# Query rotation moved to channel-major with half swaps by DMA, and the FFN input transposed by DMA, in a pre-norm attention + FFN block

## What is computed

```python
h = layernorm(x)
q, k, v, g = h @ Wq.T, h @ Wk.T, h @ Wv.T, h @ Wg.T        # each [.., 128], 8 heads of 16
q, k = rope(q), rope(k)                                    # z*cos + rotate_half(z)*sin
kv, ksum, vsum = sum_s k_s v_s^T, sum_s k_s, sum_s v_s     # per head, over the 256 tokens
num = q @ kv * scale + vsum
den = q @ ksum * scale + 256
o = (num / den + depthwise_conv5(v) + b) * g
x = x + o @ Wo.T
h2 = layernorm(x).bfloat16
y = e4m3fn(h2 / s_in) @ e4m3fn(W / s_k) * (s_in * s_k)     # FFN: one 128x128 product
out = x + bf16(y) + bias
```

## Time and profile before

| | before |
|---|---|
| median of 3 runs | 174.56 us (174.33 to 174.72) |
| the profiled execution | 174.49 us |
| its span, first to last instruction | 172.7 us |
| mean granted PE clock | 0.985 |
| PE, DVE, ACT, POOL busy | 94%, 88%, 77%, 80% of the span |
| HBM read, written | 5.25 MB, 4.19 MB |

### The profile page before, as it was taken

The page is one execution under the profiler, slowest core; times in us unless marked ns, Lnnn a source line. Parts: engine busy times, 40 slices in busy tenths (PEclk is TensorE's granted clock), DMA queues, the critical chain, the costliest instruction groups (busy, mean ns, idle before and its releaser), DMA issues.

```text
span 172.7 us, 3890 instructions
## 1 busy us (share of the span) xinstructions
PE 162.4 (94%) x1140; PEld 137.7 (80%) x1140; DVE 152.2 (88%) x281; ACT 132.5 (77%) x358; POOL 137.4 (80%) x163
## 2 busy tenths in 40 slices
PE   7999999999999999999999999999999999999730
PEld 2578988887879898998889898988998898978510
DVE  2298899989898999999899999989899899899944
ACT  3759757787987878896969888887787786667770
POOL 1468987777897888989898898996889875979871
PEclk9999999999999999999999999999999999999985
DMA  4930002004040404021030404040310220020224
GB/s 133 272 83 0 0 6 61 2 4 121 2 121 6 121 0 123 4 65 56 16 111 0 121 6 121 6 121 0 92 35 0 65 61 4 0 65 2 61 61 121
DMA packets 18966, 9.71 MB, mean 56 GB/s; under 512 B 1536, under 2 KB 18816, under 8 KB 18944
## 3 DMA queue, kind: packets, MB, share of 16 engines
q1 hardware_dynamic: 18368, 9.19, 18.6%
q10 hardware_dynamic: 576, 0.26, 0.6%
HBM read 5.25 MB, written 4.19 MB: 55 GB/s over the span
## 4 chain that ended last, share of the span: by engine, by line
PE 85%; POOL 4%; DVE 3%; issue 3%; ACT 2%; DVEq 0%; POOLq 0%; ACTq 0%
PE bank L1126 15%; PE bank L1210 9%; PE bank L1172 8%; PE p_num L1191 8%; PE bank L1137 8%; PE p_num L1183 8%; PE bank L1145 7%; PE bank L1161 4%; PE bank L1200 4%; PE bank L1116 4%; PE bank L1153 4%; PE bank L1083 3%; PE bank L1253 2%; PE bank L1219 2%; DVE yc L786 1%
## 5 line engine op out<-in xcount | busy, mean ns | idle before, releaser
L597 POOL TENSOR_TENSOR qk<-turned 128x512 f32<-128x512 f32 x32 | 40.3, 1274 | 3.1 <-DVE turned L826 2.9
L826 DVE TENSOR_TENSOR turned<-bank,turn 128x1024 f32<-128x1024 f32 x32 | 38.7, 1216 | 0.9 <-PE bank L1126 0.9
L841 DVE SCALAR_TENSOR_TENSOR acc<-bank,conv_w,acc 128x510 f32<-128x510 f32 (+1 forms) x48 | 34.8, 725 | 0.2
L1126 PE MATMUL bank<-w_qk,hT 128*128 128x256 f32 x128 | 32.8, 381 | 0.2
L370 ACT ACTIVATE h<-x,nmr,rs 128x128 bf16<-128x128 f32 x60 | 24.7, 485 | 3.9 <-POOL nmr L571 3.9
L306 ACT ACTIVATE h<-xs,nmr,rs 128x128 f32<-128x128 f32 x64 | 26.3, 484 | 0.6 <-POOL nmr L560 0.4
L557 POOL TENSOR_TENSOR rs<-ve,minus_half 128x4 f32<-128x4 f32 (+1 forms) x17 | 16.7, 980 | 12.5 <-ACT ve L297 12.5
L1126 PEld LDWEIGHTS bank<-w_qk,hT 128*128 128x128 f32 x128 | 22.6, 190 | 2.9 <-issue 0.3
L568 POOL TENSOR_TENSOR rs<-ve,minus_half 128x4 f32<-128x4 f32 (+1 forms) x17 | 16.6, 977 | 6.7 <-ACT ve L361 6.6
L609 POOL TENSOR_TENSOR acc<-acc,outer 128x508 f32<-128x508 f32 x16 | 20.3, 1271 | 1.0 <-DVE acc L841 1.0
L1137 PEld LDWEIGHTS bank<-w_v,hT 128*128 128x128 f32 x128 | 16.4, 191 | 4.7 <-issue 3.3
(11 more groups left out here) (88 smaller groups left out, 326.6 us busy)
## 6 DMA issues: line engine op xcount, KB each, us to landing
xs<-_attn_hidden_states_dram SPq DMA_DIRECT2D x15, 256.0 KB, 2.8
out_dram<-ob SPq DMA_DIRECT2D x15, 256.0 KB, 2.5
turn<-in_turn_dram SPq DMA_DIRECT2D x1, 512.0 KB, 4.7
xs<-_attn_hidden_states_dram SPq DMA_DIRECT2D x2, 128.0 KB, 2.8
out_dram<-ob SPq DMA_DIRECT2D x2, 128.0 KB, 2.1
mask<-in_mask_dram SPq DMA_DIRECT2D x1, 68.0 KB, 5.0
w_raw<-in_L_attn_Wq_dram ACTq DMA_DIRECT2D x1, 64.0 KB, 2.3
w_raw<-in_L_attn_Wk_dram ACTq DMA_DIRECT2D x1, 64.0 KB, 2.5
```

What stands on the lines that cost most here:

```text
L597: nc.gpsimd.tensor_tensor(qk[:, u % 2, j].rearrange("p q t d -> p t q d"), turned[:, j, :, :, 0:D].rearrange("p a h (q d) -> p (a h) q d", ...
L826: nc.vector.tensor_tensor(turned[:, j], p_qk[j].rearrange("p a h d -> p a (h d)").unsqueeze(2).to_broadcast([P, TPB, 2, 2 * D]), turn[:], ...
L841: nc.vector.scalar_tensor_tensor(out=part, in0=p_vT[:, :, lo + off:hi + off], scalar=conv_w[:, k:k + 1], in1=part, op0=ALU.mult, op1=ALU.a ...
L1126: last = nc.tensor.matmul(p_qk[j][:, a].rearrange("p h d -> p (h d)"), hT[:, u % 3, t * P:(t + 1) * P], w_qk[:].rearrange("p a q d -> p (a ...
```

## The change

q and k are no longer projected together. q is projected channel-major in one 128x512 product, like the gate, and rotated there. The two halves of a rotated pair now lie on different partitions (0 to 63 and 64 to 127), so DVE writes both products (z*cos and z*sin) and SP swaps the partition halves of the second by two DMAs from SBUF to SBUF (128 KB each); POOL adds them straight into `qT`. `transpose_q` and `move_qT` are gone. k stays token-major, in four 128x128 products. The table of 512 KB is loaded as two tables of 256 KB. For units 0 to 13 the bf16 `h2` (128x512, 128 KB) is transposed by a DMA of SP into a new SBUF tile `h2T`, which ACT (or DVE on the wide path) reads in place of PSUM; units 14 and 15 still use PE. The banks of PSUM are assigned anew, and the orders of all five queues are new. The code up to the orders, cut to its core:

```diff
+            def swap_q(u):
+                s = u % 2
+                sp.wait_ge(q_turned_done, count(u))
+                sp.dma_start(q_swapped[0:P // 2, s], q_turned[P // 2:P, s, 1]).then_inc(q_swapped_in[s], 16)
+                sp.dma_start(q_swapped[P // 2:P, s], q_turned[0:P // 2, s, 1]).then_inc(q_swapped_in[s], 16)
+
+            def turn_h2(u):
+                s = u % 2
+                sp.wait_ge(h2_done, count(u))
+                if u >= 2:
+                    sp.wait_ge(q8_done, count(u, 2))
+                sp.dma_start(h2T[:, s].rearrange("p (t k) -> p t k", t=TPU), h2[:, s].rearrange("p t d -> p (t d)"),
+                             transpose=True).then_inc(h2T_in[s], 16)
...
-            def move_qT(u):
...
-                    act.wait_ge(h2T_filled, count(u))
+                    if u < PE_H2:
+                        act.wait_ge(h2T_in[u % 2], h2T_count(u))
+                    else:
+                        act.wait_ge(h2T_filled, 1)
...
-            def add_rope(u, j):
...
+            def add_q(u):
+                s = u % 2
+                pool.wait_ge(q_swapped_in[s], 32 * (u // 2 + 1))
+                if u >= 2:
+                    pool.wait_ge(num_filled, count_last(u, 2))
+                nc.gpsimd.tensor_tensor(qT[:, s], q_turned[:, s, 0], q_swapped[:, s], ALU.add).then_inc(qT_done, 1)
+
+            def add_k(u):
+                s = u % 2
+                pool.wait_ge(k_turned_done, count(u))
+                if u >= 2:
+                    pool.wait_ge(kv_filled, count(u, 2))
+                nc.gpsimd.tensor_tensor(k[:, s], k_turned[:, s, :, :, 0:D // 2], k_turned[:, s, :, :, D // 2:D],
+                                        ALU.add).then_inc(k_done, 1)
...
-            def rope(u, j):
...
+            def turn_q_unit(u):
...
+                nc.vector.tensor_tensor(
+                    q_turned[:, s].rearrange("p c (j s) -> p c j s", j=BPU),
+                    p_q[:].rearrange("p (j s) -> p j s", j=BPU).unsqueeze(1).to_broadcast([P, 2, BPU, S]),
+                    turn_q[:].unsqueeze(2).to_broadcast([P, 2, BPU, S]), ALU.mult).then_inc(q_turned_done, 1)
+
+            def turn_k_unit(u):
...
+                nc.vector.tensor_tensor(
+                    k_turned[:, s].rearrange("p (j a) h d -> p j a h d", j=BPU),
+                    p_k.rearrange("p (j a) d -> p j a d", j=BPU).unsqueeze(3).to_broadcast([P, BPU, TPB, 2, D]),
+                    turn_k[:].unsqueeze(1).to_broadcast([P, BPU, TPB, 2, D]), ALU.mult).then_inc(k_turned_done, 1)
...
-            def project_qk(u, j, *freed):
+            def project_q(u, *freed):
...
+                nc.tensor.matmul(p_q[:], w_qk[:, 0].rearrange("p a d -> p (a d)"), hT[:, u % 3], start=True,
+                                 stop=True).then_inc(q_filled, 1)
+
+            def project_k(u, *freed):
...
+                for t in range(TPU):
+                    last = nc.tensor.matmul(p_k[:, t], hT[:, u % 3, t * P:(t + 1) * P],
+                                            w_qk[:, 1].rearrange("p a d -> p (a d)"), start=True, stop=True)
+                last.then_inc(k_filled, 1)
```

The middle of the orders, of PE, DVE, ACT, POOL and SP in turn:

```diff
             for t in range(7, 13):
                 project_g(t - 3, (x2_done, count_last(t - 4)))
-                project_v(t - 1, (hT_done, count_first(t - 1)))
-                project_qk(t - 1, 1, (rope_done[1], count(t - 2)))
-                transpose_t1(t - 3, (qT_done, count(t - 3)))
-                transpose_h2(t - 4, (v_done, count(t - 1)))
+                key_value(t - 2, (kvs_done, count(t - 3)))
+                transpose_t1(t - 3, (hT_done, count_first(t - 1)))
+                project_v(t - 1, (yb_done, count(t - 5)))
+                project_k(t - 1, (k_turned_done, count(t - 2)))
                 transpose_v(t - 1, (tap_done[-1], count(t - 2)))
-                key_value(t - 2, (rope_done[0], count(t - 2)))
-                ffn(t - 4, is_small, (q8_done, count(t - 4)))
-                transpose_q(t - 2, (t2_done, count_last(t - 3)))
+                project_q(t - 1, (v_done, count(t - 1)))
                 project_o(t - 3, (oT_done, count_last(t - 3)))
                 sum_v(t - 2, (t1_done, count_last(t - 3)))
-                project_qk(t - 1, 0, (kvs_done, count(t - 2)))
-                transpose_h(t, (yb_done, count(t - 4)))
                 attend(t - 2)
+                ffn(t - 4, is_small, (q_turned_done, count(t - 1)))
+                transpose_h(t, (t2_done, count_last(t - 3)))
...
+            for t in range(5, 12):
+                mask_kv(t - 2)
+                add_lepe(t - 3)
                 stats1(t)
-                add_lepe(t - 3)
                 gate(t - 3)
-                rope(t - 1, 1)
-                mask_kv(t - 2)
+                turn_k_unit(t - 1)
+                turn_q_unit(t - 1)
                 quantise_if_wide(t - 4, is_small)
                 residual(t - 3)
+                conv_tap(t - 1, 0)
                 stats2(t - 3)
...
+            for t in range(9, 12):
                 norm2(t - 4)
                 move_v(t - 1)
-                quantise_if_small(t - 4, is_small)
                 var_eps1(t)
                 conv_middle(t - 1)
+                conv_outer(t - 1)
+                quantise_if_small(t - 4, is_small)
+                norm1(t)
+                var_eps2(t - 3)
                 move_y(t - 4)
-                conv_outer(t - 1)
-                norm1(t)
-                move_qT(t - 2)
-                var_eps2(t - 3)
                 move_hT(t)
...
+            for t in range(9, 12):
+                add_k(t - 2)
+                pow2(t - 4)
                 add_bias(t - 5)
+                add_q(t - 2)
                 final_sum(t - 5)
+                pow1(t)
+                sum_outer(t - 2)
...
+            load_x(9)
+            swap_q(7)
+            turn_h2(5)
+            store(4)
+            load_x(10)
+            swap_q(8)
+            store(3)
+            turn_h2(6)
```

More of the change, by code:

```diff
@@ L217, in build @@
         h2T_filled = sem("h2T_filled")
+        h2T_in = [sem(f"h2T_in{n}") for n in range(2)]
         q8_done = sem("q8_done")
@@ L945, in _ @@
             conv_tap(2, 2)
+            turn_k_unit(3)
+            turn_q_unit(3)
             dve.wait_ge(w_ready, 1)
```

777 lines of the change are left out of this document (413 added, 364 removed).

## The result

The changed kernel was timed three times, each beside the kernel before on the same chip. First: 173.7 us (172.96 to 174.09) against 174.53, ratio 0.9951 [0.9929, 0.9972]. Then 0.9995 [0.9973, 1.0017] and 0.9951 [0.9932, 0.9970]. Two of the three ratios show it 0.5% faster, the third shows no difference; 2.3% was forecast. The profiled execution took 173.71 us, its span is 171.9.

What follows compares the result with a forecast made beforehand. PE was taken to bound the kernel at 9.445 us a unit, with DVE close behind at 9.02. From 174.49, minus 3.6 and 0.6 of DVE's waits plus 0.1 gave 170.4, as median 170.5; range 167 to 178.

Steps and rivals of the forecast that it cites:

- PE, 8.78 us a unit: Steady stage: PE, spared transposes of q and h2, falls from 9.445 to 8.78 us a unit, below DVE's 9.02.
- The pace of 9.1: Steady stage: DVE's floor of 9.02 us a unit, plus a few hundredths between dependent instructions, sets about 9.1.
- The rotations: DVE's two rotation instructions of 1024 elements in new patterns stay at 1.21 us each, at most 1.38.
- rival (b): Gain used up by costlier DVE patterns, a swap landing in 5.0 or bank 0 waits: 173 to 176, chance 0.18.
- The transpose: DMA transpose of h2 lands in 2.8 us against 2.0 of cover, so ACT waits 0.8 a unit, under 9.1.
- Rival (c): Slower through the DMA transpose on ACT: it decides from 3.9 us on, a landing of 5.0 gives 190; chance 0.20.
- The swap: POOL's add_q can run 2.8 to 3.5 us behind DVE's rotation, hidden by 4.5 us of other work.
- The tail and SP's queue: Tail's chain keeps its steps; SP issues five DMAs, some 2 us of 9; a load costs the swap at most 0.7.
- The head: Start: tables up to 0.4 and first rotation 0.3 worse, convolution 0.6 better; with the tail 0.1 us to the bad.

Runs made afterwards that it cites:

- pe_all: Changed kernel with h2 of units 0 to 12 transposed by PE in place of the DMA transpose; ratio 1.0138 to the kernel before.
- double_turn: Changed kernel with each DMA transpose of h2 preceded by a second one to a spare tile, waited for; 206.03 us, ratio 1.1772 to the kernel before.
- no_turn: Changed kernel with no transpose of h2 for units 0 to 13, the quantisation reading h2 itself; 169.74 us, ratio 0.9712 to the kernel before.
- no_swap: Changed kernel with the halves of rotated q added unswapped and the 32 swap DMAs left out; 170.27 us, ratio 0.9762 to the kernel before.
- part 4: Runs of the changed kernel with transposes of h2 delayed or left out, or swaps left out; ratios 1.1772, 0.9712, 0.9840 and 0.9762 to the kernel before.
- third execution: Third profiled execution of the unedited changed kernel; its residual of unit 0 starts at 26.11 us.
- head_order: Changed kernel with x of unit 1, Wo and the rotation's tables loaded ahead of the convolution's constants and the mask; ratio 0.9937 to the kernel before.
- pairs_adjacent: Changed kernel with DVE's statistics moved in units 5 to 11, so two dependent instruction pairs stand together; ratio 0.9941 to the kernel before.
- order_four_x: Changed kernel with SP's new tail order and POOL's wait at the end, but four buffers for x; 2.1% slower than the changed kernel.

## Why the prediction was right in sign and wrong in size

**PE, 8.78 us a unit: right**, 8.80 in the profile. **The pace of 9.1: wrong, to the good.** It took DVE's 9.02 of busy time as its floor. But busy time depends on the order: an instruction that does not read its predecessor's result starts some 0.08 us before that one's span ends, a dependent one does not, and the new order separates two such pairs. DVE is busy for 8.76 a unit with the same kinds of instructions, needs about 8.7, PE is still the bound, and the transposes moved off PE are worth their full 0.22 (pe_all). Busy time in one order is not an engine's floor in another.

**The rotations: right**, 1218 and 1215 ns. So one of rival (b)'s three causes fell away.

**The transpose: right in size, thin in cover.** It lands in 2.4 us (2.8 was taken), though SP's issue is 1.2 of it. The instruction on SP's queue, its duration in ns (least, median, most), and the landing in us:

```profile
L279 SPq DMA_TRANSPOSE h2T<-h x14: 1195/1205/1507, 33.7 to 155.1; - x14
...
DMA to landing us min/median/max: 2.4/2.4/4.1
```

In undisturbed units ACT does not wait for it, where the forecast gave it 0.8 us of wait; with a landing of 4.0 it waits 1.48, so the cover is some 2.5 (an estimate from these two) where 2.0 was said. Rival (c) put the point from which the landing decides at 3.9 us, counting ACT's spare time, and had 187 to 190 for a landing of 4.8 to 5.0. In double_turn, the run nearest to that, a unit at full clock takes 10.7, not far above the 10.4 that (c) gives for 4.8; the rest of its 206 us is PE's lower granted clock, the slow units, and SP, which stands still during the spare transpose. The estimate of 5.2 us from the Trainium skill's "VectorE: DVE Perf Modes" ("The three transpose paths") is not borne out for four tiles in one transfer: all four land in less than two of its single ones. But the forecast let each transfer land alike. Two of 14 took 4.0 and 4.1 us (5.1 for the second in another execution), and no_turn shows what one is worth: between units 5 and 6 it gains 1.5 us on the changed kernel.

**The swap: hidden from POOL, as said, but not free.** POOL waits 3.4 us for it in five places, 1.5 of that in the head. What no_swap gains comes for the greater part from unit 8 on and not through these waits (part 4).

**The tail and SP's queue: the step that failed.** The sum took the tail at nothing: "The tail's chain has the same steps." It cost 2.6 us, 1.5 between unit 10 and the last residual and 1.1 behind it. Of SP's queue the forecast said of a load that waits for the residual: "it costs the swap at most 0.7 us, inside the cover above". That was worked out for the middle, where DVE's residual comes right behind the rotation. In the tail DVE's order is another, and there the load held a ready swap for 4.0 us and helped to hold a transpose for 1.5, for which ACT waited 2.1. SP's issues take 3.2 us a unit (0.38 load, 0.51 + 0.60 swap, 1.20 transpose, 0.51 store), where some 2 were said. The tail's steps were not the same: ACT and POOL had become dependent on three more DMAs a unit. By unit 10 the lead was 3.4 us, about what the forecast's sum gives for that point, but by luck: a pace 0.3 better than said gave more, and the slow landing of unit 4 took 1.5 of it back. With the fifth buffer, SP's order and POOL's wait the stretch from unit 10 to the last residual takes 41.55 us, as in the kernel before, and the kernel is at 169.7, 0.8 below the forecast.

**The end: not seen.** In the kernel before, POOL added the bias of unit 14 at 166.61, just behind DVE's last normalisation; with unit 14's FFN earlier against the last residual it fell beside it: 1.1 us. The kernel before had its own case of this, DVE's addition at 167.99 with 1.14 in place of 0.28. **The head:** the residual of unit 0 is 1.96 later (1.3 in the third execution) where 0.1 was said for head and tail together. The first rotation starts at 11.39 (10.75) in place of 9.45, since the projection of v and Wo's transpose stand ahead of the first projection of k; with Wo loaded earlier (head_order) it starts at 10.68, hardly earlier than in the third execution. The delay is made up by unit 2, and that it costs anything at the end is not shown.

The rival that came nearest is (b), the gain used up, 173 to 176, with 0.18 where the forecast had 0.52. Its general reason, too small a margin in four engines' fixed orders, was near; its places (bank 0, the patterns, POOL) were not, so that its range holds the measured 173.7 is partly luck.

Open: why the transpose of unit 4 lands in 4.0 us in several of these kernels. A 16 KB packet of an instruction fetch comes in the same stretch in the changed kernel, at 70.9, as the last of the transpose's packets go. In pairs_adjacent such a packet comes behind the transpose (at 71.4, with the landing at 71.1), and the landing takes 2.4. That fits, but the cause was not tried. Nor was the small scatter of the kernels explained: 0.4 us from least to most in the first six runs of the kernel before, 1.1 in those of the changed one.

## What to carry to other kernels

When work is moved from an engine to DMAs, draw the issuing queue as one more engine: write down for every DMA when its source is ready and what stands ahead of it, in the head, the middle and the tail each. A load that waits for a free buffer must not stand ahead of a transfer on the path; here one more buffer brought 0.9% by itself, and the new order without it cost 2.1%, both against the changed kernel. Compare the kernels at points along the way, not only at the end: the lead was won in the middle and lost in the tail. And profile the unedited kernel more than once before a shift of 0.7 us is put down to an edit.

## What the runs showed of the hardware

- A DMA transpose of 128x512 bf16 takes SP 1.20 us to issue (median; 1.51 at most in the changed kernel), where a load mostly takes 0.37 to 0.6, and lands in 2.4 us (median; 4.1 at most); a swap by two transfers from SBUF to SBUF takes 0.51 + 0.60 to issue (medians; up to 1.4 close behind another DMA), and each lands in 2.8 (median).
- DVE's normalisation of 128x128 from f32 to bf16 took 0.34 us alone and 1.26 beside POOL's additions, and the two ended with them, to 0.1 us; its addition of 128x256 bf16 took 0.28 and 1.14. In the middle DVE's additions with one operand in PSUM stayed at 0.68 beside the same POOL instructions.
- A DVE instruction of 128x512 whose successor reads its result costs 0.11 to 0.13 us more (0.71 to 0.72 from start to start in place of 0.59 to 0.60). Part of that shows as busy time: with two such pairs a unit, DVE is busy for 8.85 of 8.95 us, without them for 8.77 of 8.80.
- PE's granted clock, 1.00 in the middle of the changed kernel, fell to 0.83 over 10 us where PE had stood idle (order_four_x, 115 to 125 us, behind a wait of 3.65 us), and to 0.78 in one unit of double_turn.
